# One block for the mixture of experts and the attention, with the first two images' queries and keys prepared between the last units of the mixture

## The reference, cut to what matters

```
x = x + attention_free_mix(norm(x))            # over the rows of an image
t = t + shared_ffn(norm(t)) + sum_e w_e(t) * expert_e(norm(t))   # MoE: 8 experts, top 2, silu(gate) * up, then down
x = x + gamma * softmax(K Q^T) V               # attention, one image at a time, 576 tokens; Q, K, V from norm(x)
t = t + switch_ffn(norm(t))                    # 16 experts, top 1, limited capacity
```

## Time and profile before

| | |
|---|---|
| time, median of 3 runs | 439.88 us (438.13 to 440.44) |
| profiled execution, its own time | 439.87 us |
| span of its instructions | 438.0 us |
| busy share of the span: PE, PEld, DVE, POOL, ACT | 82%, 70%, 62%, 39%, 35% |
| MoE block | about 102 to 210 us |
| attention block's first products with the maxima's row | 229.28 us |

### The profile page before, as it was taken

The page is one execution under the profiler, slowest core; times in us unless marked ns, Lnnn a source line. Parts: engine busy times, 40 slices in busy tenths (PEclk is TensorE's granted clock), DMA queues, the critical chain, the costliest instruction groups (busy, mean ns, idle before and its releaser), DMA issues.

```text
span 438.0 us, 6363 instructions
## 1 busy us (share of the span) xinstructions
PE 361.0 (82%) x2077; PEld 306.4 (70%) x2077; DVE 273.2 (62%) x892; ACT 152.1 (35%) x324; POOL 172.6 (39%) x188
## 2 busy tenths in 40 slices
PE   5955858967999999996477999999889785899880
PEld 5955857956888888883367999998789651793330
DVE  5836894861343343385365676867674779259997
ACT  3220163444333333331224455584553620340000
POOL 5750141003488557455000852100135666005773
PEclk9999555569999999998556799999999978699996
DMA  8940410006449455520111101111001011872335
GB/s 183 273 135 6 140 76 1 1 6 151 113 106 358 104 133 198 171 47 1 28 27 28 27 8 35 35 35 35 0 13 44 24 37 49 291 259 64 91 103 150
DMA packets 29455, 39.30 MB, mean 90 GB/s; under 512 B 4504, under 2 KB 24793, under 8 KB 29150
## 3 DMA queue, kind: packets, MB, share of 16 engines
q1 hardware_dynamic: 24910, 32.05, 26.8%
q0 software_dynamic: 1728, 3.54, 2.6%
q10 hardware_dynamic: 2784, 3.29, 2.2%
HBM read 22.92 MB, written 12.93 MB: 82 GB/s over the span
## 4 chain that ended last, share of the span: by engine, by line
PE 26%; POOL 8%; DVE 7%; issue 4%; ACT 4%; DMA 3%; POOLq 0%; SPq 0%; DVEq 0%; ACTq 0%
PE ps L1771 6%; POOL xn L1177 4%; PE ps L1739 3%; PE ps L1912 3%; PE ps L1751 2%; POOL wide L1177 2%; DVE mx L1236 2%; POOL slots L1146 2%; PE ps L1924 2%; PE ps L1758 1%; DVE K L1251 1%; PE ps L1721 1%; PE ps L1720 1%; PE ps L1719 1%; PE ps L1790 1%
## 5 line engine op out<-in xcount | busy, mean ns | idle before, releaser
L806 POOL TENSOR_TENSOR t<-wide,wstage 128x384 f32<-128x384 f32 x48 | 48.7, 1017 | 69.5 <-DMA wide<-combine_w 38.1
L927 DVE TENSOR_TENSOR h<-ps,t 128x384 f32<-128x384 f32 x48 | 26.8, 558 | 57.6 <-POOL t L806 57.5
L159 POOL TENSOR_TENSOR rstd<-sm,neg_half 128x9 f32<-128x9 f32 x10 | 18.0, 1807 | 112.3 <-DVE sm L153 112.3
L844 PE MATMUL ps<-wide,gu_w 128*128 128x384 f32 x108 | 50.9, 471 | 2.9 <-PEq L713 1.7
L900 ACT ACTIVATE wstage<-ps 128x384 f32<-128x384 f32 (+1 forms) x60 | 29.4, 489 | 66.0 <-PE ps L846 63.3
L1771 PE MATMUL ps<-V,wide 128*128 128x129 f32 x400 | 52.1, 279 | 0.0
L868 PE MATMUL ps<-h,wd 128*128 128x384 f32 x120 | 49.4, 494 | 2.9 <-DVE h L927 2.5
L1771 PEld LDWEIGHTS ps<-V,wide 128*128 128x128 f32 x400 | 49.1, 194 | 0.1
L1815 PE MATMUL ps<-ew,xTd 128*128 128x512 f32 x72 | 37.3, 655 | 3.6 <-DVE R L1484 3.5
L1484 DVE SCALAR_TENSOR_TENSOR R<-ps,dense_w,R 128x128 f32<-128x128 f32 x144 | 38.3, 343 | 1.2 <-PE ps L1815 1.1
L1236 DVE TENSOR_REDUCE mx<-ps 128x1 f32<-128x576 f32 (+1 forms) x40 | 29.8, 749 | 13.6 <-PE ps L1739 13.4
(11 more groups left out here) (248 smaller groups left out, 780.1 us busy)
## 6 DMA issues: line engine op xcount, KB each, us to landing
wide<-combine_w SPq DMA_DIRECT2D x24, 384.0 KB, 5.5
slots<-zrow SPq DMA_DIRECT2D x7, 768.0 KB, 7.1
xe<-slots SPq DMA_DIRECT2D x16, 192.0 KB, 3.9
slots<-wide ACTq DMA_DIRECT2D x16, 192.0 KB, 2.9
xall<-in_x SPq DMA_DIRECT2D x8, 288.0 KB, 6.1
out<-R SPq DMA_DIRECT2D x9, 192.0 KB, 2.2
Q<-sQK SPq DMA_DIRECT2D x8, 144.0 KB, 2.4
K<-sQK SPq DMA_DIRECT2D x8, 144.0 KB, 2.5
```

The source lines that it names most:

```text
L806: nc.gpsimd.tensor_tensor(t4[v % 2][:], cB[c % 2][:, u % NB2, :], s4[u % 2], ALU.mult).then_inc(t_ok, 1)
L844: nc.tensor.matmul(o, gu_w[0][:, w], xTH[:, at], start=True, stop=False)
```

## The change

The MoE block and the attention block become one block: the four streams of the MoE are functions (`moe_tensor` and so on) called at the head of the attention's streams. The engines no longer wait for each other between them.

Within the MoE's units, by tables of unit numbers: DVE does the statistics of group 0 in units 22 to 24 and of group 1 in 37 to 39; POOL the inverse deviations after its products of units 26 and 42; DVE the normalising of group 0 in units 30 to 32 and of group 1 in 48 to 50. PE transposes group 0's tiles after units 34, 36 and 38, and projects queries and keys of images 0 and 1, by halves of 288 columns, after units 40, 42, 44 and 46; ACT and DVE make the high and low halves and the stack in the same units; SP moves both images' rows to Q and K in the last two chunks. The bank for this is bank 4. It was the third up bank, so the up products now use two, and wait for the h of two pairs earlier. The last `back` and `residual` stand inside the first image's energies. The loop over n begins at -1. ACT runs a tiny exponential after its last silu, which loads that table there. SP clears old semaphores at the head of the MoE and not after it.

```diff
@@ tables and POOL
+        STATS_AT, RSTD_AT, NORM_AT = (22, 37), (26, 42), (30, 48)
+        FIRST_T, FIRST_QK = (34, 36, 38), (40, 42, 44, 46)
...
+                    elif u in RSTD_AT:
+                        g = RSTD_AT.index(u)
+                        pool.wait_ge(var5, g + 1)
+                        norm_rstd(GT, g, P, rs5)
...
-                for g in range(BEFORE):
-                    pool.wait_ge(var5, g + 1)
-                    norm_rstd(GT, g, P, rs5)
@@ SP
+                    if c >= CHUNKS - 2:
+                        n = c - CHUNKS + 2
+                        sp.wait_ge(k0, QK_FILLS)
+                        sp.wait_ge(sth, 2 * (n + 1))
+                        rows_to(sp, n)
@@ PE, the MoE
-                        if v >= 3:
-                            pe.wait_ge(h_ok, pair_unit(v - 3) + 1)
-                        product3(bank[2 + v % 3][:, :CH], slice((2 * k + 1) * P, (2 * k + 2) * P), tokens).then_inc(u_ps, 1)
+                        if v >= 2:
+                            pe.wait_ge(h_ok, pair_unit(v - 2) + 1)
+                        product3(bank[2 + v % 2][:, :CH], slice((2 * k + 1) * P, (2 * k + 2) * P), tokens).then_inc(u_ps, 1)
...
+                def first_transposes(c):
+                    pe.wait_ge(xn5, 1)
+                    if c:
+                        pe.wait_ge(t_lo, c)
+                    for t in range(3):
+                        last = nc.tensor.transpose(bank[4][:, t * P:(t + 1) * P], xn[0][:, 3 * c + t, :], ident)
+                    last.then_inc(t_ps, 1)
+
+                def first_qk(n, h):
+                    pe.wait_ge(t_lo, 3)
+                    if n or h:
+                        pe.wait_ge(sth, 2 * n + h)
...
+                    nc.tensor.matmul(o, gu_w[0][:, w], hT[:, at], start=True, stop=False)
+                    nc.tensor.matmul(o, gu_w[0][:, w], lT[:, at], start=False, stop=False)
+                    nc.tensor.matmul(o, gu_w[1][:, w], hT[:, at], start=False, stop=True).then_inc(qkh, 1)
...
-                back(CHUNKS - 1)
-
-            @block.scalar
-            def _(act):
+                    if u in FIRST_T:
+                        first_transposes(FIRST_T.index(u))
+                    if u in FIRST_QK:
+                        first_qk(*divmod(FIRST_QK.index(u), 2))
+                return back
@@ ACT, the MoE
+                    if u + 1 == UNITS:
+                        nc.scalar.activation(once[0:1, 1:2], konst[0:1, K_ID:K_ID + 1], ACT.Exp)
+                    if u in FIRST_T:
+                        c = FIRST_T.index(u)
+                        act.wait_ge(t_ps, c + 1)
+                        act.wait_ge(g_ps, 3 * NB2)
+                        nc.scalar.activation(hT[:, c * CH:(c + 1) * CH], bank[4][:, :CH], ACT.Copy).then_inc(t_hi, 1)
@@ DVE, the MoE
-                    if UNITS - 2 * NB2 <= u < UNITS:
-                        if u == UNITS - 2 * NB2:
-                            dve.wait_ge(R_ok, CHUNKS // 2)
-                        ahead(u - UNITS + 2 * NB2)
-                residual(CHUNKS - 1)
+                    for g in range(BEFORE):
+                        if u - STATS_AT[g] in range(3):
+                            stats(g, u - STATS_AT[g])
+                        if u - NORM_AT[g] in range(3):
+                            normalised(g, u - NORM_AT[g])
+                    if u in FIRST_T:
+                        first_low(FIRST_T.index(u))
+                    if u in FIRST_QK:
+                        first_stack(*divmod(FIRST_QK.index(u), 2))
@@ the attention's loops
-                transposes(-3)
-                for n in range(-2, B):
+                back = moe_tensor(pe)
+                for n in range(-1, B):
...
-                        if k == 0 and n + 2 < B:
+                        if k == 0 and 0 <= n < B - 2:
                             project_qk(n + 2)
+                        if k == 1 and n == -1:
+                            back(CHUNKS - 1)
```

More of the change, by code:

```diff
@@ L554, in metaformer_kernel @@
         nomax = sb("nomax", [33, SS])
+        sH = [sb(f"sH{p}", [P, SS], F32R) for p in range(2)]
+        sQK = [sb(f"sQK{p}", [P, SS], F32R) for p in range(2)]
+        NXE = 9
+        xe_all = sb("xe_all", [P, NXE * CH])
+        once = sb("once", [P, 2])
         local = ExitStack()
@@ L934, in residual, with stats @@
                                             ALU.add).then_inc(R_ok, 1)
[L936 to L945, removed]
[L946 to L951 removed]
+                def stats(g, part):
+                    if part == 0:
+                        dve.wait_ge(R_ok, 3 * (g + 1))
+                    for t in range(3 * part, 3 * part + 3):
+                        ins = nc.vector.bn_stats(st[g][:, t, :], R[:, GT * g + t, :])
+                    if part == 2:
+                        norm_moments(f, ins, GT, g, P, EPS_C, var5)
@@ new lines, in normalised, with first_low @@
+                def normalised(g, part):
+                    if part == 0:
+                        dve.wait_ge(rs5, g + 1)
+                    for t in range(3 * part, 3 * part + 3):
+                        ins = nc.vector.tensor_scalar(xn[g][:, t, :], R[:, GT * g + t, :], sm[g][:, 4, t:t + 1],
+                                                      rstd[g][:, t:t + 1], ALU.subtract, ALU.mult)
+                    if part == 2:
+                        ins.then_inc(xn5, 1)
+                def first_low(c):
+                    dve.wait_ge(t_hi, c + 1)
+                    at = slice(c * CH, (c + 1) * CH)
+                    nc.vector.tensor_tensor(lT[:, at], bank[4][:, :CH], hT[:, at].bitcast(F32), ALU.subtract).then_inc(t_lo, 1)
@@ L953, in _, with first_stack @@
+                def first_stack(n, h):
+                    dve.wait_ge(shh, 2 * n + h + 1)
+                    at = slice(h * HALF, (h + 1) * HALF)
+                    nc.vector.scalar_tensor_tensor(sQK[n][:, at], bank[4][:, :HALF], konst[:, K_SGN + 1:K_SGN + 2],
+                                                   sH[n][:, at].bitcast(F32), ALU.mult, ALU.subtract).then_inc(sth, 1)
                 f = Steps(dve, dve5)
-                for u in range(UNITS + LAG + 2):
+                for u in range(UNITS + 1):
@@ L984, in metaformer_kernel @@
         ctx.callback(local.close)
-        sH = [lsb(f"sH{p}", [P, SS], F32R) for p in range(2)]
-        sQK = [lsb(f"sQK{p}", [P, SS], F32R) for p in range(2)]
         rs = [lsb(f"rs{p}", [P, NB_SS]) for p in range(2)]
@@ L1393, in _ @@
                             maximum(n + 1, k)
-                        if k == 0 and n + 2 < B:
+                        if n == -1 and k == 1:
+                            residual(CHUNKS - 1)
+                        if k == 0 and 0 <= n < B - 2:
                             stack(n + 2)
@@ L1571, in route_exp @@
                     nc.scalar.activation(route("lx", g), route("lx", g), ACT.Exp).then_inc(ex6, 1)
-                for n in range(-3, B):
+                moe_scalar(act)
+                for n in range(-1, B):
                     g = behind(n, 4)
```

147 lines of the change are left out of this document (76 added, 71 removed).

## The result

The changed kernel takes 426.85 us (median of 4 runs, 425.83 to 428.62) against 440.16 us for the kernel before (median of 4 runs): the medians are 13.3 us apart, and the ratio on record is 0.9688, 95% interval 0.9649 to 0.9726, so about 3% faster. Predicted were 424.5 us, in a range from 420.5 to 429.5. The profiled execution took 426.19 us, with a span of 424.4 us. Measured once more beside later kernels it had a median of 426.64 us and a ratio of 0.9681 (0.9634 to 0.9728).

A forecast was written before the change was run, and what follows sets the result against it. PE bounds the MoE at full clock; at the seam one serial chain makes PE wait, then work slowly. 3.6 - 5.2 - 13.8 = -15.4 us from 439.9 gives 424.5 us, range 420.5 to 429.5.

The forecast's parts named there:

- (a): MoE up to its last gate product (T): added PE work and two up banks, 3.6 us later (3.5 to 7).
- 1.0 us at the start: MoE's first units: with two up banks the fourth up product waits for the second h, about 1.0 us (0.9 to 1.1).
- the price of nine transposes and twelve projections: Work added to PE's full stream in the MoE: 2.6 us (3.0 at most).
- the term for waits: MoE's units: waits from late h with two up banks, taken as 0, bounds 0 and 3 us.
- by the row on normalising the sum keeps 0: DVE beside POOL in the MoE: normalising kept 0.86 us, so no waits; by the port rule up to 1 us more.
- No wait that I find exceeds 1 us: MoE's units of 1.69 us: no wait found above 1 us, used against the clock falling there.
- (b): From T, the MoE's last gate product, to the last down product's end: 8.4 us now, 5.2 us less.
- (c): From the last down product's end to the landmark, image 1's energies: 21.6 us now, 13.8 us less.
- The step: Work left between last down product and image 1's energies: first energies, five maxima, residual, gap, maxima's row onward; 7.8 us.
- the first (more waits in the MoE, 6 us): MoE: h over 0.66 us late in many units, 0.3 us in each of 20, 6 us; 430.5 us; 8 in 100.
- The second: Attention's ramp: clock stays high or returns early, two or three stretches of 1.5 us less; 420 us; 6 in 100.
- The third: MoE: PE waits for a bank every unit and its clock falls to 0.50; 25 us cost, 449 us; 3 in 100.

The follow-up runs named there:

- the first experiment: The kernel before with only two up banks in place of three; one run took 439.04 us.
- dummies: The changed kernel with dummy transposes on PE where it waits in steps n = -1 and n = 0; 424.05 us (0.9602).
- the kernel with late rows: The changed kernel, but images 0 and 1's rows are moved to Q and K only after the MoE's last down product; one run took 431.77 us.

## Why the prediction was right

The mechanism held in each of its three terms, and the sum was 0.9 us too good at the landmark. That it was no more is in part luck: the terms missed by 0.6, 0.7 and 0.5 us, and the third miss went the other way.

(a) The MoE's delay was 4.2 us, not 3.6. The two parts that were worked out from rows held: 1.0 us at the start (shown by itself in the first experiment) and the price of nine transposes and twelve projections, 2.5 for the predicted 2.6 us. Mis-sized was the term for waits, which I took as 0 with a bound of 3 us: it is 1.1 us. The step that failed reads "by the row on normalising the sum keeps 0". I had a row of 0.41 us for a small operation beside t, and weighed only the normalising by it, not the chain of seven small operations. In the kernel before, group 0's chain had stood in unit 52, where nothing waited for it, and group 1's had cost 0.3 us in unit 55. "No wait that I find exceeds 1 us" held only for PE's idle time (0.86 us), not for what it cost.

(b) The tail gave 4.5 and not 5.2 us. The last `back` but one and three down products now stand in one row on PE, and the last pair starts 3.1 us after T instead of 2.4. I had placed the down products by their h alone and forgotten what PE has queued in front of them.

(c) The chain to the landmark gave 14.3 for 13.8 us. The step (7.8 us predicted, 7.3 and 6.7 measured in the two profiles) was composed of the right pieces; image 0's energies began right behind the last down product and not 0.5 us later. What the old kernel's side of (b) and (c) was worth depends on when its clock fell: by the profile of two banks alone, up to 2.4 of the 18.8 us are the clock's.

The rest, some 1 us between the landmark and the end (209.7 us against 208.8 before), is no cost of the change that the record shows: in the changed kernel's second profile the same distance is 208.6 us. It lies within what differs from one execution to the next.

Of the rivals, the first (more waits in the MoE, 6 us) came true in kind and to a fifth in size. The second did not happen by itself, but can be forced: dummies bring the 3 us. The third, a falling clock in the MoE, showed itself once, in the kernel with late rows: PE had waited 2.49 us for the first h with two banks, then worked at 0.57 in the stretch from 107 to 111 us, and unit 4's gate was 1.3 us later than in the changed kernel's second profile. It cost one short stretch and did not last, and a pause of 2.45 us at the same place in that second profile passed without a fall. The Trainium skill's report ("TensorE: Matmul & The Clock Gate", section "A second HAM failure mode: psum-queue depth-cycling") of a clock that falls again and again because of short pauses is not what the MoE's steady state does here: its granted clock is 1.00 from 110 to 206 us. But the two banks did not make PE pause in every unit either, as the rival had it; after unit 4 there is the one pause of 0.86 us. What many short pauses would do, no run here shows.

## What to carry to other kernels

A stage that keeps one engine full can carry another stage's serial start, if each moved piece is priced on the full engine and the slack of the buffer that it takes is read from the trace: here 4.2 us paid, 18.8 us won, of which up to 2.4 us may be the clock's. Give up a buffer only from the place on at which the moved work needs it; that alone was worth 2 us of the 4.2. And place small VectorE operations on SBUF in GpSimd's pauses (0.9 us here), or leave slack behind them (1.1 us here, by the third bank): nine elements can wait for most of a microsecond.

## What the runs showed of the hardware

A VectorE tensor_scalar on nine elements waits for GpSimd's fill too: 0.40 us, ending with a fill that only writes, where the operations with two SBUF inputs beside that same fill kept their 0.16 to 0.17 us. Normalising beside GpSimd's inverse deviation, 1.8 us each, kept its 0.86 us for three: it started at 202.08 us, after the second inverse deviation (202.01 to 203.86 us), and was not held. There the measurement differs from what the Trainium skill ("SBUF — State Buffer", section "Who interferes with whom") says, and decides: not every GpSimd instruction blocks it for its whole length.

TensorE's granted clock differed by execution in places where it cost nothing. In the stage from 60 to 101 us it was 0.56 in the profile of before and 1.00 in that of after, with 29.8 and 30.4 us of busy PE; POOL's first t in the MoE started at 105.61 and 105.59 us.
